# Splitting and turning the attention probabilities first in every token step

## The reference

```python
x = x + xattn(layernorm(x), ctx_768, Wq, Wk, Wv, Wo, bo)    # 8 heads of 64, 64 context rows, softmax over the 64
x = x + ffn(layernorm(x), gate_w, bias, W1, W3, W2, sw1, sw3, sw2)
# ffn: scores = sigmoid(X @ gate_w.T); the best 4 of 32 experts of each token (by scores + bias), 512 slots each;
#      silu(xe @ W1) * (xe @ W3) @ W2 per expert, weighted and added, and one shared expert for all tokens
```

## Time and profile before

| what | us |
|---|---|
| median of 3 runs (lowest, highest) | 1758.38 (1755.84, 1762.31) |
| the profiled execution | 1757.34 |
| its span | 1755.5 |
| TensorE busy | 1643.0 (94%) |
| VectorE busy | 1359.3 (77%) |
| ScalarE busy | 1148.2 (65%) |
| GpSimd busy | 1124.1 (64%) |

### The profile page before, as it was taken

The page is one execution under the profiler, slowest core; times in us unless marked ns, Lnnn a source line. Parts: engine busy times, 40 slices in busy tenths (PEclk is TensorE's granted clock), DMA queues, the critical chain, the costliest instruction groups (busy, mean ns, idle before and its releaser), DMA issues.

```text
span 1755.5 us, 32521 instructions
## 1 busy us (share of the span) xinstructions
PE 1643.0 (94%) x9061; PEld 1021.2 (58%) x9061; DVE 1359.3 (77%) x3651; ACT 1148.2 (65%) x2496; POOL 1124.1 (64%) x978
## 2 busy tenths in 40 slices
PE   5999999999999999999999999999977999999997
PEld 4555566556655656565666656555534555555554
DVE  4678787878888788888888788888875777777775
ACT  4777777777777777777777777777643444444442
POOL 1327777767777777777777777777766454444455
PEclk8999999999999999999999999999998999999999
DMA  8758977765665566655656656666646876688852
GB/s 298 192 133 231 220 174 168 168 156 128 136 146 138 129 135 150 146 143 128 141 137 132 133 130 145 138 144 165 134 94 191 222 197 162 163 200 198 200 140 25
DMA packets 466888, 277.01 MB, mean 158 GB/s; under 512 B 341839, under 2 KB 384079, under 8 KB 466708
## 3 DMA queue, kind: packets, MB, share of 16 engines
q1 hardware_dynamic: 407316, 244.99, 54.7%
q0 software_dynamic: 59392, 29.94, 10.7%
HBM read 135.06 MB, written 223.08 MB: 204 GB/s over the span
## 4 chain that ended last, share of the span: by engine, by line
PE 34%; DVE 24%; ACT 17%; issue 15%; DMA 5%; SPq 3%; ACTq 1%; DVEq 0%; POOL 0%; POOLq 0%
PE GE_ps L1572 6%; PE UE_ps L1572 6%; PE O_ps L484 5%; PE YE_ps L1610 4%; PE S_ps L469 3%; ACT done L841 3%; DVE top_s L1297 3%; DMA pt_l<-p_l 3%; PE G_ps L511 2%; DVE x_l L1238 2%; DVE S_ps L1303 2%; ACT xt_h L751 2%; SPq L394 2%; ACT xr L851 2%; ACT waste L704 2%
## 5 line engine op out<-in xcount | busy, mean ns | idle before, releaser
L929 POOL DMA_INDIRECT slot_rows<-xr,slot x480 | 517.2, 1078 | 132.6 <-issue 125.8
L1559 POOL DMA_INDIRECT out<-ye,token x128 | 198.9, 1554 | 207.5 <-DMA out<-ye,token 90.3
L939 POOL TENSOR_TENSOR xt_l<-xt,xt_h 128x512 fp32r<-128x512 f32 x128 | 163.9, 1281 | 204.4 <-ACT xt_h L751 204.2
L792 ACT ACTIVATE prob<-S_ps,rs 128x512 f32<-128x512 f32 x128 | 88.1, 688 | 248.7 <-DVE S_ps L1303 248.7
L484 PE MATMUL O_ps<-m_h,pt_h 128*128 128x512 f16 x512 | 197.9, 386 | 43.1 <-DMA pt_l<-p_l 41.9
L469 PE MATMUL S_ps<-a_h,xt_h 128*128 128x512 f32 x512 | 212.1, 414 | 2.4 <-DVE m_l L1276 2.4
L469 PE MATMUL S_ps<-a_h,xt_l 128*128 128x512 f32 x512 | 201.3, 393 | 0.0
L469 PE MATMUL S_ps<-a_l,xt_h 128*128 128x512 f32 x512 | 201.0, 393 | 0.0
L484 PE MATMUL O_ps<-m_h,pt_l 128*128 128x512 f16 x512 | 196.5, 384 | 0.0
L484 PE MATMUL O_ps<-m_l,pt_h 128*128 128x512 f16 x512 | 196.3, 383 | 0.0
L954 POOL TENSOR_TENSOR prob<-prob,rsum 128x512 f32<-128x512 f32 x128 | 134.9, 1054 | 70.0 <-DVE rsum L1331 68.1
(11 more groups left out here) (257 smaller groups left out, 4636.1 us busy)
## 6 DMA issues: line engine op xcount, KB each, us to landing
rows<-slot_rows SPq DMA_DIRECT2D x128, 280.0 KB, 3.4
xt<-in_xT SPq DMA_DIRECT2D x128, 256.0 KB
xr<-in_x SPq DMA_DIRECT2D x64, 512.0 KB, 4.0
out<-done SPq DMA_DIRECT2D x64, 512.0 KB, 3.2
up_more<-in_w SPq DMA_DIRECT2D x36, 256.0 KB, 4.4
slot_rows<-xr SPq DMA_DIRECT2D x16, 560.0 KB, 5.6
slot_rows<-xr,slot POOLq DMA_INDIRECT x512, 3.2
up_w<-in_w SPq DMA_DIRECT2D x28, 256.0 KB, 4.6
```

Source lines behind the costliest of these rows:

```text
L792: act.activation(prob[:, t % 2, :, :], S_ps[t % 2][:, :].rearrange("p (h j) -> p h j", h=H), ACT.Exp, scale=rs[:, q % 2, 0, t % 2:t % 2 + ...
L929: pool.indirect_dma_start(slot_rows, bass.IndirectOffsetOnAxis(ap=slot[:, g % 2, i, q:q + 1], axis=0), xr[:, t % (4 * XRING), :], None, bo ...
L939: pool.tensor_tensor(xt_l[:, t % 2, :, :], xt[:, t % 2, :, :], xt_h[:, t % 2, :, :].bitcast(F32), ALU.subtract).then_inc(xt_lo, 1)
L1559: pool.indirect_dma_start(out, bass.IndirectOffsetOnAxis(ap=token[:, e % RING, c:c + 1], axis=0), ye[:, e % 4, c, :], None, bounds_check=T ...
```

## The change

In every token step the probabilities of tile n-9 move ahead. On ScalarE `p_h` becomes the first operation of the step (after two that occur in a single step each), ahead of the split of the input tile, the prepared chunk and the second normalisation. On VectorE `p_l` moves from between the subtraction and the sums to ahead of the low part of the prepared chunk. On SyncE the two turns of the probabilities are issued ahead of the turns of the rows in all steps, and so ahead of the fills of the first steps. What the operations compute, their number and their shapes stay the same.

```diff
@@ SyncE, step(n)
                     t = at(n, MIX)
-                    if t is not None and t >= FINAL - 1:
+                    if t is not None:
                         turn_probabilities(t)
                     t = at(n, X2)
                     if t is not None:
                         turn_rows(t)
                     if 1 <= n <= E // 2:
                         fill_first(n)
-                    t = at(n, MIX)
-                    if t is not None and t < FINAL - 1:
-                        turn_probabilities(t)
@@ ScalarE, step(n)
+                    t = at(n, MIX)
+                    if t is not None:
+                        act.wait_ge(prob_done, t + 1)
+                        after(act, p_turned, t * 32)
+                        act.activation(p_h[:, :], prob[:, t % 2, :, :].rearrange("p h j -> p (h j)"), ACT.Copy,
+                                       scale=P_SCALE).then_inc(p_hi, 1)
                     t = at(n, XT_SPLIT)
...
                     if t is not None:
-                        rows_scaled(t)
-                        if n < TAIL - 1:
-                            rows_high(t)
+                        normal_rows(t)
 
                     m = roots_at(n)
...
-
-                    t = at(n, MIX)
-                    if t is not None:
-                        act.wait_ge(prob_done, t + 1)
-                        after(act, p_turned, t * 32)
-                        act.activation(p_h[:, :], prob[:, t % 2, :, :].rearrange("p h j -> p (h j)"), ACT.Copy,
-                                       scale=P_SCALE).then_inc(p_hi, 1)
-                    if n == TAIL - 1:
-                        rows_high(FINAL - 4)
@@ VectorE, step(n)
                     roots(n, 0)
+                    if s9 is not None:
+                        low_probabilities(s9)
                     b, j = chunk_at(n, 2)
...
-                    if s13 is not None and n < TAIL - 1:
-                        rows_low(s13)
-                    if n == TAIL - 1:
-                        low_probabilities(s9)
+                    if s13 is not None:
                         rows_low(s13)
...
                     roots(n, 3)
...
-                    if s9 is not None and n < TAIL - 1:
-                        low_probabilities(s9)
                     roots(n, 4)
```

## The result

The changed kernel takes 1823.76 us (median of 4 runs, 1821.59 to 1825.51) against 1760.35 us (4 runs) before: ratio 1.0357, 95% interval 1.032 to 1.0393. It is slower by 63 us; the forecast was 1803, +45.5 on the profiled execution. The profiled execution took 1823.07 us with a span of 1821.3. From 300 to 1180 us, in the middle of the tokens, the granted clock of TensorE is 1.00 before and 0.99 after, so a slower clock is not what made the steps longer.

The account below looks back on a forecast made before the run. The prediction took a serial loop through ScalarE, VectorE and the Exp to bound the tokens. 65.5 (p_h) - 4 (marking steps) - 16 (ScalarE's waits for TensorE) = +45.5 us on 1757.34: 1803 us, range 1776 to 1828.

Parts of the forecast that it names:

- The loop through ScalarE and VectorE: Token steps: ScalarE's first operations, VectorE's work to the subtraction, and the Exp run in series and set the step's length.
- the operation at the head: p_h, moved in front of ScalarE's operations in the loop: claimed to cost 0.52 us per step.
- first rival: TensorE bounds the tokens, so its 41.9 us of waits are the gain: 1715 us; chance 9%.
- The stretch on which the forecast rests: 600 to 760 us of the profile, where the chain names VectorE and ScalarE and TensorE not at all.
- its own case: The forecast proper, +45.5 us to 1803 us, with 1776 to 1815 us as its part; chance 69%.
- second rival: GpSimd closes a tighter loop, its product releasing p_h: 64 marking and slot steps grow further, +19, 1823 us; chance 15%.
- the rival's clause: Marking and slot steps: scatters or low parts meet VectorE's moved operation, one takes 0.5 us longer; 64 steps grow 0.3 us.
- -4 us: Marking steps, taken at +0.4 us each: 32 x 0.12 = 4 us less than the sum for ScalarE.
- the bound of +0.6: Upper end of a marking step's cost, put between -0.2 and +0.6 us.
- 16 of 23.4 us: ScalarE's waits for TensorE, 23.4 us together: two thirds counted as won back, -16 us, bounds 0 and -23.4.
- The third rival: Marking and slot steps absorb the shift; 32 us come in, 23.4 are got back: +9, 1766 us; chance 7%.
- 65.5: ScalarE: p_h at the step's start delays the rows' high part, 126 x 0.52 = 65.5 us more.

Follow-up runs that it names:

- neutral operation: Kernel before plus one extra ScalarE operation of p_h's size, reading a constant, ahead of the input split in each of 128 steps: 1818.54 us, ratio 1.0332.
- the shadow: Kernel before plus the same extra ScalarE operation, placed behind p_h and ahead of the Exp, where ScalarE waits for VectorE's subtraction: 1757.15 us, ratio 0.9978.
- the run in which they are 44.1 us: Changed kernel with VectorE's p_l back between the subtraction and the sums; p_h and the turns stay first: 1820.95 us, ratio 1.0356.
- the exchange: Kernel before with GpSimd making the hidden values' low part ahead of the input tile's low part: 1740.19 us, ratio 0.9891.
- SyncE's part alone: Kernel before with only the probabilities' turns issued ahead of the rows' turns and the fills on SyncE: 1761.7 us, ratio 1.0021.

## Why the prediction was right, and where it was off

The mechanism held. The loop through ScalarE and VectorE bounds the tokens: the operation at the head costs 0.50 to 0.52 us in plain, slot and undisturbed routing steps (the last from 9.75 to 10.27 us), and a neutral operation in its place costs 56.5 us in all, nothing in the shadow. The waits for the turned probabilities went and gave the loop back only what ScalarE had waited for TensorE. The forecast's first rival, TensorE as the bound, is refuted by the change itself, which ended those waits and took 63 us more, by the run in which they are 44.1 us and the time is the changed kernel's, and by the neutral operation. The stretch on which the forecast rests was a favourable one, though. From 600 to 760 us the chain before holds no TensorE, but from 300 to 1180 us it does (`O_ps` 5.8%, `S_ps` 3.6%, `G_ps` 2.8%), and the exchange ran into it at once: TensorE was never far behind.

That the measured time lies in the range of 1776 to 1828 owes something to luck. It is outside the part that the forecast gave to its own case (1776 to 1815) and on the second rival's 1823 (1803 and 19 make 1822). That rival went another way. `p_h` waits only 2.8 us for GpSimd's product from 60 us on, and GpSimd's split came first in only two of 24 marking steps. What did come true is the rival's clause that a low part of GpSimd meets VectorE's moved operation and takes half a microsecond longer, but in the marking steps alone, and through `member` and `x_l`, not through `p_h`. The two misses below, 16 and 6 us, happen to come near the rival's 19.

The size was 18 us too small, and the term that was mis-sized is the marking step's. I had put -4 us for 32 of them. An undisturbed one went from 9.94 to 10.84 us, 0.90 (0.84 in the mean) in place of the 0.40 that I took, outside the bound of +0.6 that I gave: (0.90 - 0.40) x 32 = 16 us. I had seen that `nt` would slip through ahead of GpSimd's split and that `p_l` and the split would tie. What I weighed was the split blocking `p_l`. It went the other way round: `p_l` was first by 0.06 us, held the split up by half a microsecond, that pushed `ht_l` back, and `ht_l` then blocked `member` or `x_l`. With `p_l` at its old place the mean marking step is 10.42 us after 10.06 before, and there the split takes 1.27 us; so 0.36 us of the growth go with `p_h` and 0.48 with `p_l`.

The rule that I cited, in the Trainium skill, SBUF — State Buffer, Who interferes with whom, says that a VectorE instruction with two inputs in SBUF and a GpSimd instruction that reads SBUF exclude each other and that the first one holds on to its end. The traces agree with that: `p_l` 1.34 us behind `ht_l`, GpSimd's split 1.80 us behind `p_l`, each with the other's end inside it. `member` has one input, so that sentence does not cover it; that it is held up too is what the trace shows. What I lacked was the second step, who stands behind the one that is held up.

The gain from TensorE's waits I had put at 16 of 23.4 us. ScalarE got back 23.1 of them, but waits 13 us more for VectorE's hidden values, so by an estimate about 10 us are left; an operation that had been late together with another is not early because the other is. Of the rows' turns I had said only that TensorE needs them a step later; SyncE's part alone shows that ScalarE's next row split waits for them as well, though not in the whole change. The third rival, marking and slot steps that absorb the shift, was wrong for both kinds. These terms do not close to the last microsecond: 65.5 + 12 - 10 makes 67.5 with the marking steps at +0.38 above the others, 64.5 us is the growth up to the last input split, and I did not follow the rest.

## What to carry to other kernels

An engine that is busy 94% and waits 42 us for one input can still be off the path most of the time; before an operation is moved to end such a wait, ask in which engine's wait it now stands, and price its new place by what queues behind it. When ScalarE waits for VectorE once per step and VectorE for ScalarE once per step, the operations ahead of each wait are the step's length, and those inside the waits are free. A GpSimd operation that holds up VectorE's is better placed in GpSimd's own idle time, which here gave 1.1% by exchanging two of them.

## What the runs showed of the hardware that was not expected

A VectorE operation that normally takes a fraction of a microsecond can be held up by one of GpSimd's: `before`, with 32 elements to a partition, took 0.67 us and `member` up to 1.34 us beside GpSimd's low parts, and `x_l` 1.75 us in place of 0.68. So what stands ahead of the prediction, that engines wait for each other by counting semaphores alone, is not the whole of it. The blocked engine shows it as a longer instruction, not as an idle time, so no view of waits lists it; it is found by comparing the durations of one line over the steps. A delay of half a microsecond given to GpSimd came back to VectorE through GpSimd's next instruction.
